# A GNN layer and a product-key attention layer on one core: the dense head's passes one step further ahead

## The reference, cut to what matters

```python
# per head: two sets of 128 sub-keys, 16 best of each, then the 16 best of the sums
scores, idx = top_k(sim, 16)
score = scores[0][..., :, None] + scores[1][..., None, :]
final_scores, pk_idx = top_k(score, 16)
final_scores = softmax(final_scores)
k = einsum('bnhk,bnhkd->bnhd', kv_scores, keys_table[ind])      # 16 rows of 16384, weighted
v = einsum('bnhk,bnhkd->bnhd', kv_scores, values_table[ind])
sim = where(causal, einsum('bihd,bjhd->bhij', q, k), neg)
out = einsum('bhij,bjhd->bhid', softmax(sim), v)                # then @ Wo, residual
```

## Time and profile before

| | |
|---|---|
| median of three runs | 15474.37 us |
| the profiled execution | 15469.79 us |
| its span | 15468.0 us |
| mean granted TensorE clock | 0.781 |
| busy, share of the span | PE 59%, PE weight load 44%, DVE 47%, POOL 44%, ACT 32% |
| DMA | 98 GB/s, 20.6% of 16 engines for the gathers, 10.7% for loads and stores |
| PE busy in comb, turn, multiply | 938.2, 1578.5, 4824.0 us |

### The profile page before, as it was taken

How to read it: one execution, slowest core, us unless ns; L and a number is a source line. 1 busy time by engine, 2 the same in 40 slices (tenths; PEclk the granted TensorE clock), 3 DMA queues, 4 the chain that set the end, 5 groups by cost and what they waited for, 6 DMA issues and landing times.

```text
span 15468.0 us, 181213 instructions
## 1 busy us (share of the span) xinstructions
PE 9127.0 (59%) x51232; PEld 6871.9 (44%) x51232; DVE 7216.5 (47%) x32006; ACT 4929.6 (32%) x14163; POOL 6782.6 (44%) x7177
## 2 busy tenths in 40 slices
PE   4556555555665555656555565655655555565655
PEld 3444444444444444444444444444444444444444
DVE  5444444444444444444444444444444454444443
ACT  2333333333333333333333333333333333333333
POOL 3444444444444444444444444444444444444444
PEclk7777787777777777778777777777877777777777
DMA  3333333333333333333333333333333333333332
GB/s 92 101 98 102 97 100 95 102 101 93 100 94 103 100 96 97 98 98 103 93 99 97 96 102 95 98 99 98 104 95 101 97 98 101 99 94 98 94 101 90
DMA packets 445985, 1516.88 MB, mean 98 GB/s; under 512 B 123760, under 2 KB 141552, under 8 KB 379248
## 3 DMA queue, kind: packets, MB, share of 16 engines
q0 software_dynamic: 344064, 939.98, 20.6%
q1 hardware_dynamic: 100848, 564.37, 10.7%
HBM read 1499.66 MB, written 4.19 MB: 97 GB/s over the span
## 4 chain that ended last, share of the span: by engine, by line
PE 33%; another core or an unknown queue 30%; DVE 16%; issue 12%; ACT 8%; DVEq 0%; ACTq 0%; DMA 0%; SPq 0%
PE dense_ps L459 14%; DVE wide L1099 6%; PE wideT_ps L445 5%; ACT expo L692 3%; ACT wideT L627 3%; PE score_ps L495 2%; PE comb_ps L567 2%; PE probT_ps L501 2%; PE front_ps L399 2%; PE score_ps L435 1%; DVE hits L1062 1%; PE comb_ps L426 1%; PE score_ps L483 1%; DVE neg L1109 1%
## 5 line engine op out<-in xcount | busy, mean ns | idle before, releaser
L334 POOL DMA_INDIRECT got<-in_table,rows x7168 | 6780.6, 946 | 8648.6 <-PE comb_ps L567 6404.0
L459 PE MATMUL dense_ps<-tab,wideT 128*128 128x256 f32 x16384 | 4824.0, 448 | 11.8 <-issue 11.7
L445 PE MATMUL wideT_ps<-ident,wide 128*128 128x128 f32 x8192 | 1578.5, 324 | 5024.0 <-ACT wideT L627 2570.7
L459 PEld LDWEIGHTS dense_ps<-tab,wideT 128*128 128x128 f32 x16384 | 3609.7, 232 | 560.2 <-issue 14.6
L445 PEld LDWEIGHTS wideT_ps<-ident,wide 128*128 128x128 f32 x8192 | 1049.9, 162 | 5781.7 <-issue 3988.4
L1099 DVE SCALAR_TENSOR_TENSOR wide<-const_ps,rank,expo 128x128 f32<-128x128 f32 x8192 | 2303.7, 344 | 1403.3 <-remote 541.9
L692 ACT ACTIVATE expo<-sim_d,shift 128x128 f32<-128x128 f32 x8192 | 2595.4, 393 | 0.6 <-DVEq L1043 0.2
L1121 DVE SCALAR_TENSOR_TENSOR acc<-probT_ps,prob_inv,acc 128x128 f32<-128x128 f32 x448 | 157.2, 351 | 3234.8 <-PE probT_ps L501 3015.8
L627 ACT ACTIVATE wideT<-wideT_ps 128x512 f32<-128x512 f32 x2048 | 1217.8, 595 | 1250.6 <-remote 671.1
L627 ACT ACTIVATE probT<-probT_ps 128x128 f32<-128x128 f32 (+3 forms) x512 | 224.0, 437 | 3890.8 <-remote 2776.2
L567 PE MATMUL comb_ps<-got,spread 128*32 128x256 f32 x14336 | 938.2, 404 | 12.3 <-issue 12.2
(11 more groups left out here) (156 smaller groups left out, 8065.9 us busy)
## 6 DMA issues: line engine op xcount, KB each, us to landing
tab<-in_dense SPq DMA_DIRECT2D x512, 1024.0 KB
got<-in_table,rows POOLq DMA_INDIRECT x7168
adj_i<-in_adj SPq DMA_DIRECT2D x16, 1024.0 KB
x_in<-in_x SPq DMA_DIRECT2D x16, 256.0 KB
out<-fin SPq DMA_DIRECT2D x16, 256.0 KB
tab<-in_wqpk_t SPq DMA_DIRECT2D x1, 512.0 KB, 10.6
tab<-in_keys_t SPq DMA_DIRECT2D x1, 512.0 KB, 15.5
wq_sb<-in_wq SPq DMA_DIRECT2D x1, 512.0 KB, 14.1
```

The costliest lines, as they stand in the source:

```text
L334: pool.indirect_dma_start(out=got[t % 2][:, g, :], out_offset=None, in_=table, in_offset=bass.IndirectOffsetOnAxis(ap=rows[buf(h)][:, t * ...
L445: mm = pe.transpose(wideT_ps[:, q * P:(q + 1) * P], wide[k % 2][:, q, :], ident[:, :])
L459: mm = pe.matmul(dense_ps[:, v * 2 * D:(v + 1) * 2 * D], wideT[k % 2][:, (2 * u + v) * P:(2 * u + v + 1) * P], tab[(k // CHUNK) % 2][:, (2 ...
```

## The change

PE multiplies pass k - 2 ahead of turning pass k. DVE weighs pass k + 1 in the place of pass k, and ACT raises pass k + 2. Pass 0 is weighed, and pass 1 raised, ahead of the first batch. The copy of the dense sums moves to the place of pass 2 of a half, where the last multiply of the half before is done. The two slots with few passes that held the left-over dense attention tiles move from 0 and 1 to 1 and 2, with the tiles, and `query_dense` from slot 2 to slot 3. At the end of the last batch two multiplies are left over instead of one.

```diff
-MIDDLE = [FEW] * 2 + [ONE] * 13 + [FEW] * 2 + [ONE] * 11
-ENDING = [FEW] * 2 + [SIX] * 13 + [FEW] * 2 + [SIX] * 2 + [ONE] * 6 + [NONE] * 3
+MIDDLE = [ONE] + [FEW] * 2 + [ONE] * 12 + [FEW] * 2 + [ONE] * 11
+ENDING = [SIX] + [FEW] * 2 + [SIX] * 12 + [FEW] * 2 + [SIX] * 2 + [ONE] * 6 + [NONE] * 3
...
-LEFT = {0: 2, 1: 3}
+LEFT = {1: 2, 2: 3}
...
         def passes(b, k0, count, first):                 # PE
             for k in range(k0, k0 + count):
+                if k >= 2:
+                    multiply(b, k - 2)
+                elif not first:
+                    multiply(b - 1, PASSES + k - 2)
                 turn(b, k)
-                if k:
-                    multiply(b, k - 1)
-                elif not first:
-                    multiply(b - 1, PASSES - 1)
...
-                if n == 2:
+                if n == 3:
                     query_dense(b)
                 if last and n == SLOTS - 3:
+                    multiply(b, PASSES - 2)
                     multiply(b, PASSES - 1)
...
         def passes(b, k0, count, first, last):           # ACT
             for k in range(k0, k0 + count):
+                if k == HALF_PASSES + 2:
+                    take_dense(b, 0)
+                if k == 2 and not first:
+                    take_dense(b - 1, 1)
                 if k:
                     take_wideT(b, k - 1)
                 elif not first:
                     take_wideT(b - 1, PASSES - 1)
-                if k + 1 < PASSES:
-                    raise_(b, k + 1)
+                if k + 2 < PASSES:
+                    raise_(b, k + 2)
                 elif not last:
-                    raise_(b + 1, 0)
-                if k == HALF_PASSES:
-                    take_dense(b, 0)
-                if k == 0 and not first:
-                    take_dense(b - 1, 1)
+                    raise_(b + 1, k + 2 - PASSES)
...
             raise_(0, 0)
+            raise_(0, 1)
...
+        def weigh(b, k):                                  # DVE
+            m = b * PASSES + k
+            half = k // HALF_PASSES
+            if k % HALF_PASSES == 0:
+                after(link(dve.tensor_copy(count_ps, count_sb[:, :, :])))
+            dve.wait_ge(expo_ready, m + 1)
+            dve.wait_ge(wideT_ready, past(m - 1))
+            for u in range(2):
+                for v in range(2):
...
+            last.then_inc(wide_ready, 1)
+
+        def passes(b, k0, count_, last):
             for k in range(k0, k0 + count_):
...
+                if k + 1 < PASSES:
+                    weigh(b, k + 1)
+                elif not last:
+                    weigh(b + 1, 0)
...
                 take_sum(0, 0, g)
+            weigh(0, 0)
             restart()
```

More of the change, by code:

```diff
@@ L1086, in take_sum @@
             dve.sem_inc(sum_taken, 1)
-        def passes(b, k0, count_, first):
-            for k in range(k0, k0 + count_):
[L1090 to L1101, removed]
-                last.then_inc(wide_ready, 1)
+        def weigh(b, k):
[7 more added lines that the diff above has]
+                for v in range(2):
+                    key = (2 * k + u) % NKEYS
+                    last = dve.scalar_tensor_tensor(
+                        wide[k % 2][:, 2 * u + v, :], count_ps[:, v, :], rank1[:, 2 * half + v, key:key + 1],
+                        expo[k % 2][:, 2 * u + v, :], ALU.is_gt, ALU.mult)
+            last.then_inc(wide_ready, 1)
+        def passes(b, k0, count_, last):
+            for k in range(k0, k0 + count_):
+                if k + 1 < PASSES:
+                    weigh(b, k + 1)
+                elif not last:
+                    weigh(b + 1, 0)
             return k0 + count_
@@ L1180, in batch @@
                 a = attend_no(b, n, 0, first, last)
-                k = passes(b, k, w[0], first)
+                k = passes(b, k, w[0], last)
                 hit_part(0)
@@ L1195, in batch @@
                     norm_scale(x_in, b * 2 + 2)
-                k = passes(b, k, w[1], first)
+                k = passes(b, k, w[1], last)
                 hit_part(1)
@@ L1207, in batch @@
                     gnn_msg(b + 1)
-                k = passes(b, k, w[2], first)
+                k = passes(b, k, w[2], last)
                 negate(a, t)
@@ L1224, in batch @@
                     norm_scale(x2, b * 2 + 3)
-                k = passes(b, k, w[3], first)
+                k = passes(b, k, w[3], last)
                 hit_part(3)
@@ L1232, in batch @@
                     rank_dense(of_d, half, 1)
-                k = passes(b, k, w[4], first)
+                k = passes(b, k, w[4], last)
                 if more and t % 2 == 1:
```

## The result

The changed kernel takes **14935.99 us**, median of 3 runs (14915.85 to 14954.72), against 15474.37: ratio 0.9656, 95% interval 0.9632 to 0.9679. The forecast was 14950. The profiled execution spans 14934.2 us.

A forecast was written before the change was run, and what follows sets the result against it. The tail from the end of the gathers' stretch to the next comb was taken as the bound. Gains of 355 us (even t) and 230 (odd t), less 64, make 520 off 15469.8: 14950 us; 8-in-10 range 14650 to 15520.

The forecast's parts named there:

- The place of the gain: PE's tail before the next comb: the fourth pass's multiply leaves it, running free behind comb while gathers run; 520 us.
- Rival D: During gathers: PE really executes slowly, so the multiply moved there costs what it saved; 15470 us, chance 0.10.
- Price of M3, even t: Tail of even-t slots: without the fourth pass's multiply, 2.3 or 1.4 us gained, mean 1.85, 355 us in all.
- The clock term: Values, project and comb: run slower without that multiply; 1.1 us lost where the tail is at half clock, otherwise 0.3.
- My 2.3 to 2.8 us for comb: Sign in the profile after: comb behind a full slot takes 2.3 to 2.8 us.
- rival B: Tail and comb: only short pieces remain, comb runs wholly at half clock, 1.93 us more; 15320 us, chance 0.12.
- Odd t: Odd-t slots: PE's move waits for DVE's later lift, limiting gain to 1.8 us, 1.2 after slower comb; 230 us.
- PE's waits on DVE's wide mostly vanish, and that pays for the M ahead of T0; I count both zero, because T3 has the whole quiet stretch: Behind comb: 730.4 us of waits mostly vanish, offsetting the earlier multiply; the fourth turn has time during gathers; net zero.
- Rival A: Tail: the fourth turn falls into it, 2.1 us a slot lost; 15920 us at three quarters of slots, chance 0.13.
- Rival C: Turns: PE no longer waits on DVE and ACT, all come earlier; 885 us less, 14590 us, chance 0.08.
- The sum: Whole kernel: even slots 355 us plus odd 230, less 64 for seams, 520 us gained, giving 14950 us.
- the seam term: Ends of dense-work halves: a new half's first multiply waits for kv_d, 2 us each, 32 times, 64 us lost.

The follow-up runs named there:

- experiment 2: Kernel before with only ACT and DVE running one pass further ahead, PE's order kept: 15633.73 us, ratio 0.9828.
- set 3: Third set of runs: kernel before 15866.17 us, changed kernel 15440.51 (0.9733), turn first with edit 1 15023.55 (0.9477).
- turn first: Changed kernel with four wideT buffers, PE turning before multiplying in a slot's first four places: ratio 0.9313; with edit 1 0.9208 and, in set 3, 0.9477.
- experiment 4: Changed kernel with the pass of the fifth place moved behind the next comb: 16209.51 us, ratio 1.0185.
- edit 1: Changed kernel with DVE's sum_rows and lift ahead of its last weigh in slots with odd t: 15403.78 us, ratio 0.9686.
- experiment 7: Changed kernel with a 512-column memset and a wait behind each gather, to spread the gathers: 16901.88 us, ratio 1.6616.

## Why the prediction was right

**The place of the gain: right, and half of it.** The tail bounds the slot, M3 left it, and the cover behind comb held in the main. Rival D would have had the slots grow by what was moved in; punctual slots with even t shrank by 2.0 us. POOL's wait came to 5905, forecast about 5800. The end of the stretch stayed 25.5 us after comb at t = 0 (the median of the punctual slots, as in both slots read), but at t = 1 to 3 it moved from about 25.7 to between 26.4 and 26.6. It hangs on the gathers: ACT reads probT 3.8 to 4.1 us after the last gather's start in the punctual slots of both kernels (medians by t), and from first to last start the gathers take 20 us instead of 19 in 45 of 84 such slots with t = 1 to 3, before in 48 of 170. Why that is more frequent is open.

**Price of M3, even t: right.** Forecast 1.85 us a slot; measured in punctual slots 31.45 - 29.45 = 2.0 and 33.44 - 31.39 = 2.05, and over all regular even slots, with the late ones, 32.51 - 30.94 = 1.57. The clock term was 1.1 us where the tail is cold. In the slot read it is 3.25 - 1.93 = 1.32 for comb and next to nothing for values and project (1.73 us from values to comb, before 1.67): the sum right, its parts not. The comb behind a five-pass slot grew from 1.95 to 2.26 us on average, and POOL's first gather went from 3.07 to 3.27 us behind comb's start, in the mean of all slots of twelve batches. My 2.3 to 2.8 us for comb is met in the mean behind slots with t = 0 and 1 (2.53 and 2.50), not behind t = 2 and 3 (2.08 and 1.93), and it hides two kinds: behind late slots, where M2 is in the tail, comb takes 1.93 to 2.10 on average, and behind punctual ones 2.67, 3.34, 2.44 and 1.93. So the 27 punctual slots with t = 1 do pay 1.41 of rival B's 1.93.

**Odd t: the chain right, one piece missing.** Lifted ends 6941.89 + 0.69 = 6942.58, 4.2 us after probT is read (6938.39); I had worked out 4.25. But the move runs in the cold tail too: it stands 6944.46 - 6942.64 = 1.82 us ahead of comb, with its 8 matmuls taking 1.89 us, where I had let it be over in 0.9 as before. Punctual slots gained 0.63 (t = 1) and 1.29 (t = 3), all regular odd slots 36.59 - 35.47 = 1.12, forecast 1.2.

**"PE's waits on DVE's wide mostly vanish, and that pays for the M ahead of T0; I count both zero, because T3 has the whole quiet stretch": this step failed.** Its first half held: T2's median start is 9.0 us behind comb, before 8.9. But T3 had not the whole stretch. In the kernel before it was already late in 29% of the five-pass slots (23% of the regular ones), which I had not counted; the one slot that I followed from comb to comb has t = 0, where it never is. The lead alone makes the regular late slots punctual and gains 1.7% (experiment 2); in the kernel before of set 3 those slots are 2.5, 1.9 and 0.1 us longer than punctual ones at t = 1, 2 and 3, 189 us or 1.2% in all. With M3' ahead of T0 to T2 late slots became more instead: 55% after. Of the slots whose T2 starts 8.2 to 9.4 us behind comb, 109 of 230 are late in the changed kernel, 1 of 70 in the one before, and none of 106 in turn first; in set 3 164 of 236 in the changed kernel and 6 of 48 in the one before. What differs is what PE was given since comb: three multiplies ahead of T2, in the others two. (With three in experiment 4 it is 59 of 197.) The lag of a signal so seems to grow with the work issued ahead of it in the stretch, as a backlog would, and not with the time alone. That would be a milder form of rival D, in which late is what PE is, not only its signals; no run tells the two apart.

**Rival A: its condition came true, its price did not.** I wrote that it decides from about 45% of the slots, and that T3 after the last gather in most slots would prove me wrong. 55% are late (77% in set 3), and the kernel is still 3.4% (2.7%) faster. I had put a late slot at 2.1 us over a slot of before, and so 3.7 over a punctual one of after. Measured in regular slots it is 1.1 and 1.6 us over a punctual one at t = 1 and 2, nothing at t = 0 (4 slots) and 0.5 less at t = 3; in set 3 1.2 to 1.9. Two terms were wrong. The slower comb (0.6) doesn't come there, since M2 in the tail brings the clock back: in the last slot of the fence above T3 to comb takes 6.98 us, 1.0 more than T4 to comb in the earlier trace rows, and the comb behind it 1.93. And I forgot that a late slot of before has M3 in its tail as well and loses it (34.60 to 33.94, 34.19 to 33.00, 39.14 to 36.89).

**Rival C: its mechanism is real.** The lead, with which PE hardly waits for DVE's wide (180.6 us in experiment 2), is worth 1.7%, half to two thirds of what the changed kernel gains (3.4% and 2.7%); I had it at zero. It did not come on top, since the new order spends it again. With turn first both are kept, and the ratio is 0.9477 instead of 0.9733; 0.5% of that may be edit 1.

**The sum: its total is partly luck.** The middle batches, counted slot by slot and carried over to 16, give 539 us (the spans 534):

```
us gained                        forecast   measured
21 regular slots a batch              507        449
slots 0 to 2 and 15 to 18              14         90
```

In the second row the forecast is that of its three five-pass slots, 78, less 64 for the seams. The first row is the M3 terms, 1.51 us a slot forecast. The late slots cost 69 us before and 108 after in it (late less punctual at the same t, over 16 batches), so the two terms that I had set to zero come to 39 us net here; without them a slot gains 1.45. In set 3 the same costs are 189 and 386 us, 197 net, 158 more than here; the ratio of 0.9733 instead of 0.9656 is worth some 120. In the second row the seam term failed: I had taken 64 us off for the seams and nothing for the slots with two passes. Slots 15 and 16 did become longer (1.3 and 5.3 us), but 17 and 18 shorter by 5.6 and 5.0; slots 15 to 18 together gain 63 us and 0 to 2 gain 27. Why, no run shows. So 534 us against 520 rests on a forecast of 58 too many in the first row and 76 too few in the second.

## What to carry to other kernels

Read more than one slot of a repeated pattern before a term is set to zero: count in how many of them the wait falls on either side of the event that decides, here T3 against the last gather. When another engine answers late for a known stretch, issue first what others must read (turns, transposes), and behind it what only fills PE (multiplies); with a multiply ahead of each turn the signals came later still. A move of order and a longer lead should be run apart as well as together: here they paid 2.1% and 1.7%, the two together 2.7% (3.4% in the first comparison), and turn first with the same lead 5.2%, of which lift first may be 0.5.

## What the runs showed of the hardware that was not expected

The quiet stretch is not a property of the kernel. The kernel before took 15474.37, 15911.86 and 15866.17 us in three sets of runs, and 10170.56 and 10170.11 us in two others; one chip gave 10170.56 and then 15866.17. Recorded durations are the same in both kinds (the 7168 gathers 6784.4 us in an execution of the changed kernel without the stretch, 6779.2 and 6796.8 with it). What differs is when others receive PE's signals while gathers run: the copy of wideT waits for a releaser without a name 3158.5 us in one and not at all in the other. Where the stretch is there, it ends about 4 us after the last gather starts (medians of 3.8 to 4.3 us in the punctual slots of the six traces of the kernel before, the changed kernel, the lead alone and turn first). Within a kernel's executions in a set of runs nothing of it varies (7 runs from 15844.99 to 15883.74). What sets it is open: experiment 7, which was to change the gathers' density, met the kind without it.

The ratio of the change depends on it: 0.9656, 0.9733 and, without the stretch, 0.9407. A verdict on the order of work in this kernel therefore holds for the kind of execution it was taken in; here the sign was the same in both.
